# First attention of a four-stage block: queries and keys turned in 32 x 32 blocks on VectorE and rearranged by a trip through memory, made one step ahead

## The reference, cut to what matters

```python
q = (hidden_states @ Wq).reshape(B, Sq, H, D)
k = (encoder_hidden_states @ Wk).reshape(B, Skv, H, D)
v = (encoder_hidden_states @ Wv).reshape(B, Skv, H, D)
q = rmsnorm(q, gq)
k = rmsnorm(k, gk)
scores = jnp.einsum('bqhd,bkhd->bhqk', q, k) * scale
attn = jax.nn.softmax(scores, axis=-1)
out = jnp.einsum('bhqk,bkhd->bqhd', attn, v)
return out.reshape(B, Sq, H * D) @ Wo
```

## Time and profile before

| | us |
|---|---|
| median of 3 runs | 2024.33 (2022.95 to 2024.97) |
| the profiled execution's own time | 2025.97 |
| its span, first to last instruction | 2024.2 |
| PE busy over the span | 1987.6 (98%) |
| DVE, ACT, POOL busy over the span | 1290.1, 795.2, 529.6 |
| first attention, steps 1 to 31 | from about 47 to about 782 in the span |

### The profile page before, as it was taken

How to read it: one execution, slowest core, us unless ns; L and a number is a source line. 1 busy time by engine, 2 the same in 40 slices (tenths; PEclk the granted TensorE clock), 3 DMA queues, 4 the chain that set the end, 5 groups by cost and what they waited for, 6 DMA issues and landing times.

```text
span 2024.2 us, 33384 instructions
## 1 busy us (share of the span) xinstructions
PE 1987.6 (98%) x12656; PEld 1642.4 (81%) x12656; DVE 1290.1 (64%) x2265; ACT 795.2 (39%) x2371; POOL 529.6 (26%) x579
## 2 busy tenths in 40 slices
PE   6999999999999999999999999999999999999999
...
GB/s 229 56 6 5 8 5 11 79 27 26 28 53 48 58 34 100 42 84 6 57 37 123 59 20 21 17 17 21 46 53 73 156 173 197 190 205 156 202 160 162
DMA packets 76487, 154.16 MB, mean 76 GB/s; under 512 B 8816, under 2 KB 31088, under 8 KB 76400
## 3 DMA queue, kind: packets, MB, share of 16 engines
...
...
## 4 chain that ended last, share of the span: by engine, by line
PE 89%; DVE 4%; DMA 2%; issue 2%; ACT 1%; POOL 1%; DVEq 0%; ACTq 0%; POOLq 0%; SPq 0%
PE four_banks L48 35%; PE bank L48 35%; PE four_banks L338 4%; PE bank L1467 3%; PE four_banks L393 3%; PE four_banks L1538 2%; PE bank L1564 1%; PE bank L1576 1%; PE bank L408 1%; PE four_banks L408 1%; DVE l_rotB L1943 1%; PE four_banks L1555 1%; DVE l_roped L1951 1%; DMA xres<-in_wq 1%; PE bank L338 1%
## 5 line engine op out<-in xcount | busy, mean ns | idle before, releaser
L2363 POOL DMA_INDIRECT m_ring<-in_table,m_row x128 | 125.7, 982 | 372.1 <-DVE l_x_all L2476 272.0
L48 PE MATMUL four_banks<-l_yT_hi,m_hi 128*128 128x512 f32 x512 | 199.4, 389 | 0.0
L48 PE MATMUL four_banks<-l_yT_lo,m_hi 128*128 128x512 f32 x512 | 199.2, 389 | 0.0
L1133 DVE TENSOR_SCALAR f_relu<-bank,f_b 128x512 f32<-128x512 f32 x64 | 47.9, 749 | 161.5 <-ACT f_h_hi L1076 161.5
L513 ACT ACTIVATE prob<-four_banks,mx,rms 128x128 f32<-128x128 f32 x256 | 114.0, 462 | 88.1 <-DVE mx L648 88.1
L1076 ACT ACTIVATE f_h_hi<-bank,f_b 128x512 fp32r<-128x512 f32 x64 | 44.1, 690 | 255.6 <-PE bank L48 255.6
L289 POOL TENSOR_TENSOR rms<-ssq,constants 128x8 f32<-128x8 f32 x64 | 13.2, 206 | 433.3 <-ACT junk L498 263.6
L2340 ACT ACTIVATE m_act_of<-m_dot,l_ln_y 128x2 f32<-128x2 f32 x64 | 18.9, 296 | 238.6 <-DVE m_junk L2466 238.6
L48 PEld LDWEIGHTS four_banks<-l_yT_hi,m_hi 128*128 128x128 f32 x512 | 96.1, 188 | 20.1 <-issue 0.2
L48 PEld LDWEIGHTS four_banks<-l_yT_lo,m_hi 128*128 128x128 f32 x512 | 96.1, 188 | 20.0
L291 POOL TENSOR_TENSOR rms<-rms,constants 128x8 f32<-128x8 f32 x64 | 105.0, 1641 | 5.0
...
## 6 DMA issues: line engine op xcount, KB each, us to landing
f_stage<-in_w POOLq DMA_DIRECT2D x14, 512.0 KB, 4.4
f_x_in<-x SPq DMA_DIRECT2D x18, 256.0 KB, 2.8
...
x_in<-in_x SPq DMA_DIRECT2D x16, 256.0 KB, 2.7
x<-xres SPq DMA_DIRECT2D x16, 256.0 KB, 2.0
x<-l_x_all SPq DMA_DIRECT2D x16, 256.0 KB, 2.0
m_stage<-in_gate SPq DMA_DIRECT2D x8, 512.0 KB, 6.2
m_stage<-in_up SPq DMA_DIRECT2D x8, 512.0 KB, 7.2
```

What stands on the lines that cost most here:

```text
L48: mm = pe.matmul(out, st, mv, start=first and n == 0, stop=last and n == len(terms) - 1)
L1133: dve.tensor_scalar(relu[m % 2][:], bank[HB[m % 2]][:], b12[:, layer, m:m + 1], 0.0, ALU.add, ALU.max).then_inc(S["relu_ready"], 1)
L2363: pool.indirect_dma_start(ring[slot][:], None, table, bass.IndirectOffsetOnAxis(ap=row[:, tile_of(g), k:k + 1], axis=0)).then_inc(S[f"got{ ...
```

## The change

Queries and keys are no longer turned on PE. DVE turns each of the 4 x 4 blocks of 32 x 32 of a head (`dve.transpose`) into a tile `blocks[g]` of [128, 4, 32, 8]: the four heads' queries and the four heads' keys lie side by side, so an element of one head is followed by the same element of the next head, and the elements of one head stand eight floats, 32 bytes, apart. The queries are turned straight from PSUM (`turn_q`); the keys are first multiplied by their inverse norm and by the gains (`norm_and_turn_k`: four `scalar_tensor_tensor` of [128, 128], then the transpose). The blocks still lie in the wrong partitions. SP writes `blocks[g]` to a DRAM tensor `turned[g]` (`send`, 512 KB, rows of 4 KB), waits until it has landed, and loads it back with the blocks exchanged into `qkT[g]` (`bring`, 512 KB, rows of 1 KB). `score` reads one head of `qkT[g]` with the step of eight floats, as stationary and as moving operand.

Queries and keys of step s + 1 are made in step s, so all loops are shifted: x is normalised two steps ahead, the context is split two steps ahead. The copies `copy_q`, `copy_kT` and `copy_qT` are gone, and so are PE's `turn_q` and `turn_k`. The inverse norms of queries and keys are taken apart (`mean`: four calls for a step, on four columns each, instead of two on eight). The squares of the queries are read from PSUM. PE's new order in a step is score 0, output 1 of the previous step, score 1, keys 0 of the next step, turn_p 0, keys 1, mix 0, queries 0, turn_p 1, queries 1, mix 1, output 0, turn_x (for s + 2), values 0, values 1. SP's is the load of the context, the store, the load of x, then send 0, bring 0, send 1, bring 1. The second half's weights are split by POOL and in other places than before, and the ffn's work in the last steps is placed anew.

```diff
-    q_sb = [sb(f"q_sb{g}", [P, G * D], F32) for g in range(2)]
-    k_sb = [sb(f"k_sb{g}", [P, G * D], F32) for g in range(2)]
...
+    k_sb = sb("k_sb", [P, G * D], F32)
+    blocks = [sb(f"blocks{g}", [P, 4, 32, 2 * G], F32) for g in range(2)]
+    qkT = [sb(f"qkT{g}", [P, 4, 32, 2 * G], F32) for g in range(2)]
...
+    gains, gk_in = (sb(n, [P, D], F32) for n in ("gains", "gk"))
...
+        def send(s, g):
+            sp.wait_ge(*at(f"k_blocks{g}", s))
+            sp.wait_ge(*at(f"q_blocks{g}", s))
+            sp.dma_start(turned[g].rearrange("p (j b) r -> (p j) (b r)", b=4), blocks[g][:].rearrange("p b i h -> p (b i h)")
+                         ).then_inc(S["qk_stored"], 16)
+
+        def bring(s, g):
+            sp.wait_ge(S["qk_stored"], 16 * (2 * s + g + 1))
+            sp.dma_start(qkT[g][:].rearrange("d p i h -> d p (i h)"), turned[g].rearrange("p d r -> d p r")
+                         ).then_inc(S[f"qk_loaded{g}"], 16)
...
-            if second_half and there(s + 2):
-                load_x(s + 2)
-            if now == STEPS - 1:
-                ahead["loads"](sp, now)
+            if there(s + 2):
+                load_ctx(s + 2)
             if storing:
...
+            if second_half and there(s + 3):
+                load_x(s + 3)
+            if now is not None and AHEAD_FROM <= now:
                 ahead["loads"](sp, now)
-            if there(s + 2):
-                load_ctx(s + 2)
...
+            if there(s + 1):
+                send(s + 1, 0)
+                bring(s + 1, 0)
...
+            if there(s + 1):
+                send(s + 1, 1)
+                bring(s + 1, 1)
...
-        def means(s, g):
-            r = rms[g]
-            both = ssq[g][:].rearrange("p a h -> p (a h)")
-            pool.wait_ge(*at(("k_squared0", "q_squared1")[g], s))
-            pool.tensor_tensor(r[:, 1, :], both, constants[:, 0, :], ALU.add).then_inc(S[f"eps_added{g}"], 1)
-            pool.wait_ge(*at(f"eps_added{g}", s))
-            pool.tensor_tensor(r[:, 0, :], r[:, 1, :], constants[:, 1, :], ALU.pow).then_inc(S[f"rms_ready{g}"], 1)
+        def mean(s, g, of):
+            own = slice(0, G) if of == "q" else slice(G, 2 * G)
+            pool.wait_ge(*at(f"{of}_squared{g}", s))
+            pool.tensor_tensor(rms[g][:, 1, own], ssq[g][:, 0 if of == "q" else 1, :], constants[:, 0, own], ALU.add
+                               ).then_inc(S["eps_added"], 1)
+            pool.wait_ge(S["eps_added"], 4 * s + (0 if of == "k" else 2) + g + 1)
+            pool.tensor_tensor(rms[g][:, 0, own], rms[g][:, 1, own], constants[:, 1, own], ALU.pow).then_inc(S[f"{of}_rms{g}"], 1)
...
+            if now == NB - 1:
+                split_lo(pool, "wq1", 1)
+                fetch("wo1", 1, after=[("wq1", 2)])
+            if now == NB:
+                split_lo(pool, "wo0", 1)
+            if there(s + 1):
+                mean(s + 1, 0, "k")
+                mean(s + 1, 1, "k")
+            if now == NB - 2:
+                split_lo(pool, "wk0", 1)
+                split_lo(pool, "wk1", 1)
+                fetch("wq1", 1, after=[("wk0", 2), ("wk1", 2)])
+            if now == NB - 1:
+                split_lo(pool, "wv0", 1)
+                split_lo(pool, "wv1", 1)
             if now is not None and AHEAD_FROM < now < STEPS:
...
+            if there(s + 1):
+                mean(s + 1, 0, "q")
...
+            if there(s + 1):
+                mean(s + 1, 1, "q")
+            if now == NB - 2:
                 split_lo(pool, "wq0", 1)
-                fetch("wq1", 1, after=[("wq0", 2)])
-                split_lo(pool, "wv0", 1)
-            if there(s):
-                means(s, 1)
-            if now != FIRST and there(s + 1):
-                split_ctx(s + 1)
-            if roots and now != FIRST:
-                root(s + 2)
+                fetch("wo0", 1, after=[("wq0", 2)])
+            if now == NB:
+                split_lo(pool, "wo1", 1)
+            if roots:
+                root(s + 3)
+            if there(s + 2):
+                split_ctx(s + 2)
             if now == 0:
...
-                pe.wait_ge(*at("ctx_split", 0))
+            if g == 0:
+                pe.wait_ge(*at("ctx_split", s))
+            elif there(s - 1):
+                pe.wait_ge(*at("v_copied1", s - 1))
...
+            if g == 1:
+                pe.wait_ge(*at("k_blocks1", s))
...
-        def turn_q(s, g):
-            if g == 0:
-                pe.wait_ge(*at("q_copied0", s))
-            elif there(s - 1):
-                pe.wait_ge(*at("y_added", s - 1))
-            turn((1, 0)[g], q_sb[g], f"q_turned{g}")
-
-        def turn_k(s, g):
-            pe.wait_ge(*at(f"k_normed{g}", s))
+            product(pe, bank[(6, 5)[g]][:], pairs).then_inc(S[f"v_made{g}"], 1)
+
+        def score(s, g):
+            pe.wait_ge(S[f"qk_loaded{g}"], 16 * (s + 1))
             if g == 1:
-                pe.wait_ge(*at("exped0", s))
+                pe.wait_ge(*at("q_squared1", s))
             elif there(s - 1):
                 pe.wait_ge(*at("oT_lo1", s - 1))
-            turn((6, 1)[g], k_sb[g], f"k_turned{g}")
-
-        def score(s, g):
-            if g == 0:
-                pe.wait_ge(*at("qT_copied0", s))
-            pe.wait_ge(*at(f"kT_copied{g}", s))
+            for j in range(G):
+                rows = qkT[g][:].rearrange("d p i h -> d (p i) h")
+                mm = pe.matmul(bank[(1, 3)[g]][:, j * P:(j + 1) * P], rows[:, :, j], rows[:, :, G + j], start=True, stop=True)
+            mm.then_inc(S[f"scored{g}"], 1)
+
+        def turn_p(s, g):
+            pe.wait_ge(*at(f"normed{g}", s))
+            if g == 0 and there(s - 1):
+                pe.wait_ge(*at("y_added", s - 1))
...
+        def mix(s, g):
+            pe.wait_ge(*at(f"pT_copied{g}", s))
+            pe.wait_ge(*at(f"v_copied{g}", s))
...
-                ahead["hidden1"](pe, 0, 4)
+                score(s, 0)
             if there(s - 1):
                 output(s - 1, 1)
             if there(s):
-                score(s, 0)
-                if now == STEPS - 1:
-                    ahead["turn_x"](pe, 0, 3)
-                if now == 0:
-                    values(0, 0)
-                values(s, 1)
+                score(s, 1)
+            if now == STEPS - 1:
+                ahead["turn_x"](pe, 0, 3)
+            if now == FIRST:
+                turn_x(0)
+            if there(s + 1):
+                keys(s + 1, 0)
+            if there(s):
+                turn_p(s, 0)
+            if there(s + 1):
+                keys(s + 1, 1)
             if now == STEPS - 1:
                 ahead["hidden1"](pe, 0, 0)
+            if there(s):
+                mix(s, 0)
             if there(s + 1):
                 queries(s + 1, 0)
...
             if there(s):
-                turn_q(s, 1)
-                turn_k(s, 1)
-            if there(s + 1) and not (isinstance(s, int) and s == FIRST):
-                values(s + 1, 0)
+                turn_p(s, 1)
...
+            if there(s + 1):
+                queries(s + 1, 1)
             if there(s):
...
-                turn_q(s + 1, 0)
+                mix(s, 1)
...
             if there(s):
-                mix(s, 0)
+                output(s, 0)
...
+            if there(s + 2):
+                turn_x(s + 2)
+            if there(s + 1):
+                values(s + 1, 0)
+                values(s + 1, 1)
...
+        def square(s, g, of):
+            act.wait_ge(*at(f"k_made{g}" if of == "k" else f"q_blocks{g}", s))
+            if of == "q" and g == 1:
+                act.wait_ge(*at("q_squared0", s))
+            made = bank[((7, 3) if of == "q" else (4, 5))[g]]
...
+                exps(s, 0)
...
+                split_hi(act, "wq1", 1)
...
+                exps(s, 1)
             if now == 0:
-                copy_v(0, 0)
+                split_hi(act, "wo0", 0)
+            if now is not None and AHEAD_FROM < now <= AHEAD_FROM + 4:
+                ahead["split_hi"](act, now - AHEAD_FROM - 1)
...
+            if there(s + 1):
+                square(s + 1, 0, "k")
+                square(s + 1, 1, "k")
...
+            if now == NB - 2:
+                split_hi(act, "wk0", 1)
+                split_hi(act, "wk1", 1)
+            if now == NB - 1:
+                split_hi(act, "wv0", 1)
+                split_hi(act, "wv1", 1)
...
+                split_o(s, 0)
+            if there(s + 1):
+                square(s + 1, 0, "q")
...
+            if there(s + 1):
+                square(s + 1, 1, "q")
+            if now == NB - 2:
+                split_hi(act, "wq0", 1)
             if now in (0, NB):
                 split_hi(act, "wo1", now // NB)
...
+            if there(s):
+                split_o(s, 1)
...
+            if there(s + 2):
+                split_xT(s + 2)
+            if now == NB - 1:
+                split_hi(act, "wo0", 1)
+            if there(s + 1):
+                copy_v(s + 1, 0)
+                copy_v(s + 1, 1)
...
+            if there(s + 2):
```

(58 more changed lines are left out.)

316 lines of the change are left out of this document (99 added, 217 removed).

## The result

The changed kernel takes 2103.51 us (median of 4 runs, 2102.01 to 2105.00) against 2024.22 us of the kernel before (4 runs, 2022.95 to 2024.97) on the same chip: a ratio of 1.0392, 95% interval 1.0374 to 1.0410. It is slower by 79 us, and the forecast was 1992 with a range up to 2048.

What follows compares the result with a forecast made beforehand. PE was taken to bound the kernel before; after the change, the chain through memory would set a 21.7 us step. 2024.2 - 47 (steady gain) + 14 (unhidden work) = 1991 of span, runs 1992; range 1968 to 2048 with rivals.

Steps and rivals of the forecast that it cites:

- PE's work without the transposes, 21.27: PE's work in a first-attention step once turn_q and turn_k (1.76 us) are removed: 21.27 us.
- The score operands, taken at 0.89: Four score products reading operands at a 32-byte step were to take 0.89 us, as with contiguous operands.
- upper bound of 1.78: Most that four score products with 32-byte-step operands were to take: twice the 0.89 us of before.
- The rival with these operands: Strided score operands double in price: PE 23.05 us a step above a 22.6 chain, total 2027; chance 0.17.
- DVE's transposes, taken at 0.69: Each DVE transpose of 512 columns was to take 0.69 us, as a copy; upper bound 3.36.
- The key product, four in 1.1: DVE's four multiplications of keys by inverse norm and gains, on the chain: 4 x 0.27 = 1.1 us.
- the rest of the chain to blocks 0, 10.1: ACT's and DVE's work from score 1's start until blocks 0 is ready to send: 10.1 us.
- The trip, 11.3: SP's send 0, bring 0, send 1, bring 1 in sequence, until bring 1 lands: 11.3 us.
- send 1 beside bring 0: Send 1, sharing the DMA engines with bring 0, was to land 1.0 us behind it, at 7.6.
- Other work in the chain, 14: Weight splits and step 0 no longer hidden: 4.2 us in steps 25 to 28, 6 around 15, 4 in step 0.
- the slow trip: Rival: the trip through memory is longer, each extra microsecond costing 32 in all; 2 extra give 2055; chance 0.22.
- the forecast's lower end: Total if nothing waited but PE: 2024 - 61 + 5 = 1968 us.

Runs made afterwards that it cites:

- e6: e5 without the store to memory and the load back, score reading the blocks tile directly (not the reference's result): 1981.14 us, ratio 0.9791.
- e1: Changed kernel with score reading 128 neighbouring elements per operand, other elements than the reference asks for: 2068.45 us, ratio 1.0225.
- e3: Changed kernel with queries and keys in separate parts, queries at a 16-byte step, keys in runs of 32 elements, 512-byte pieces: 2086.56 us, ratio 1.0308.
- e4: Changed kernel with each head's 128 rows neighbouring after the bring, which fetches 4096 pieces of 128 bytes: 2069.77 us, ratio 1.0223.
- e5: e1 with the transposes also writing runs of 32 neighbouring elements, pieces still 1 KB (not the reference's result): 2030.74 us, ratio 1.0036.
- e7: e5 with half of the bytes in each store and load back from step 1 on (not the reference's result): 1989.35 us, ratio 0.9822.
- e13: Changed kernel without the loads of the second half's attention weights, their splits kept (not the reference's result): 2101.62 us, ratio 1.0383.
- e14: Changed kernel without loads and without splits of the second half's attention weights (not the reference's result): 2090.62 us, ratio 1.0317.
- e9: Changed kernel with the ffn's split_hi moved behind split_o 1 on ACT in steps 25 to 28: 2089.23 us, ratio 1.0308.
- e15: e12 with normalise 1 placed ahead of the key product of keys 0 again on DVE: 1981.70 us, ratio 0.9787.
- e11: Changed kernel with two heads interleaved (8-byte step) and each exchange cut in two, transfers of 256 KB: 2008.51 us, ratio 0.9913.
- e10: Changed kernel with 8-byte step, ACT and DVE work ahead of the trip reordered, ffn's split_hi later, separate squares' scratch tile: 2035.86 us, ratio 1.0047.
- e12: e11 with the order of e10: 1996.54 us, ratio 0.9854.

## Why the prediction was wrong, step by step

- **PE's work without the transposes, 21.27.** Right: 21.40 in e6. PE as the bound of the kernel before was right too.
- **The score operands, taken at 0.89.** This step failed, and is worth 35 of the 111 us by which the time is above the forecast (e1). A group takes 1.92, beyond even the upper bound of 1.78. The reason given, that each instruction already spends twice the time of a dense column and so has time to spare for its reads, was wrong: the weight load went from 191 to 332 ns, and it paces the group (e3). The rival with these operands had score 1's excess both in PE's work (23.05) and on the chain (22.6), but it took all else as forecast and ended at 2027: it didn't ask what else the same step of 32 bytes would slow. The rule of the Trainium skill, Advanced Engine Details and Errata, section Memory Cachelines (two hits on a 16-byte line), is borne out at three points: 332 ns at a step of 32 bytes, 327 at 16, 196 to 205 at 8. DVE's transposes follow it in their output: from PSUM 1122 ns at 32, 1080 at 16 and 698 at 8, and from SBUF 1192 at 32 and 713 at 8.
- **DVE's transposes, taken at 0.69.** This term was mis-sized for the same cause. The lower bound, a copy, had a neighbouring output; with one, the transposes take 0.67 to 0.71 (e4, e5), and with the change's output step 1.12 to 1.19. Two lie on the chain, 0.9 a step; e1 to e5, where the transposes' output alone changes, is 38 us. The Trainium skill, VectorE: DVE Perf Modes, section The three transpose paths, gave an estimate of 1.24; the 1.12 to 1.19 of this kernel look like it, but e5's 0.70 shows that as a price of the transpose it would be too high.
- **The key product, four in 1.1, and the rest of the chain to blocks 0, 10.1.** Right: 1.12, and 10.2 and 10.3 in e4 and e5, where the operands don't interfere.
- **The trip, 11.3.** 12.16. The term that was short is send 1 beside bring 0: 4.2 until bring 1 is issued was forecast, 5.05 measured. Send 0 took 2.65 where 3.1 was forecast, and bring 1 to score 1 took 3.99 where 3.5 was. The estimate of two transfers that share the engines came from two loads issued 0.4 apart. Here a store runs beside a load for most of its length, and e7 shows that it is long by what the two carry. Score 0 was to find its operands a microsecond early; in the changed kernel it waits about 0.1 for them in a steady step.
- **Other work in the chain, 14.** 41 less the 4 that the kernel before had. Step 0 was right (6.3, which is 3.7 over the 2.6 of before; the forecast had 4). Steps 14 to 17 cost 15.4 where 6 was forecast, by their splits (e13 and e14). Steps 25 to 28 cost 16.2 where 4.2 was: the forecast counted the split and not the load that the split releases, which runs into send 0 (e9). On top, the clock fell after long waits, which the forecast had not priced (below), and the step that ends in step 6 has 2.4 of which the forecast knew nothing.
- **The sum.** A chain of 22.4 plus 0.9 plus 1.0 is 24.3, against 24.43 measured. The forecast gave the slow trip, the operands and the transposes chances of 0.22, 0.17 and 0.06 as if one of them would come. They lie on one chain and add, all three came, and the range ended at 2048, between the 2036 and the 2055 that single ones of them led to. The small slips in its arithmetic don't matter: 23.02 - 1.76 is 21.26 and not 21.27, the terms of bias to blocks 0 add up to 8.17 and not 8.1, and 1991.2 + 1.8 - 1.6 is 1991.4 and not 1992.

What the whole was worth, from the changed kernel down, taken in this order: score's operands 35 us (e1), the transposes' output 38 (e5), the trip with its late steps 50 (e6). PE's work alone is not 1968, as the forecast's lower end had it, but 1981 (e6): 8 of the 13 lie in the steps that end in steps 15 to 17, which take 23.0 to 25.4 there.

e15 beats e11 by 27 us, and none of it is steady: both steps are 21.5. In the traces 9.4 us lie in the steps that end in steps 15 to 17, where the ffn's split plays no part, so that is the new order; 8.4 lie in steps 25 to 28, where the order and the later split were changed together in e10, e12 and e15, and their shares stay open.
